# Moving the final normalisation of a fused attention and feed-forward kernel from VectorE to ScalarE and GpSimd, on one core

## The reference, cut to what matters

```python
xn   = layernorm(x)                                        # no gain, no bias
q, k, v = split(xn @ Wqkv + bqkv)
qp, kp  = elu(q) + 1, elu(k) + 1
attn = (qp @ (kp.T @ v)) / (qp @ sum(kp) + 1e-6)           # per sequence
z    = layernorm(xn + attn) * g1 + b1
h    = silu(z @ Wg + bg) * (z @ Wu + bu)                   # 256 -> 682
y    = layernorm(z + h @ Wd + bd) * g2 + b2                # 682 -> 256
gate = silu(scale * (xn @ ternary(W).T))
out  = x + y * gate
```

## Time and profile before

| what | value |
|---|---|
| time, three runs | 1328.03 us median (1326.86, 1328.03, 1335.59) |
| profiled execution, span from first to last instruction | 1331.0 us; its own time is not shown apart from the three above |
| PE / PEld busy | 1285.1 us (97%) / 1152.5 us (87%) |
| DVE busy | 1159.3 us (87%), 2900 instructions |
| ACT busy | 940.7 us (71%) |
| POOL busy | 632.6 us (48%), 683 instructions |
| TensorE clock granted, mean | 0.993 |
| transfers | 41 GB/s over the span |

### The profile page before, as it was taken

How to read it: one execution, slowest core, us unless ns; L and a number is a source line. 1 busy time by engine, 2 the same in 40 slices (tenths; PEclk the granted TensorE clock), 3 DMA queues, 4 the chain that set the end, 5 groups by cost and what they waited for, 6 DMA issues and landing times.

```text
span 1331.0 us, 25237 instructions
## 1 busy us (share of the span) xinstructions
PE 1285.1 (97%) x8147; PEld 1152.5 (87%) x8147; DVE 1159.3 (87%) x2900; ACT 940.7 (71%) x1626; POOL 632.6 (48%) x683
## 2 busy tenths in 40 slices
PE   7889999999999999999999999999999999999995
PEld 5779898898898989889888888888989888988884
DVE  6987888989888988988989888989888988878886
ACT  5697777777777877677777677777677777756641
POOL 4732444554534554544554544554543554533343
PEclk8999999999999999999999999999999999999998
DMA  6200011111011111011111011111001111111100
GB/s 195 80 17 17 1 49 49 49 48 49 9 41 48 49 49 49 6 43 49 49 49 48 17 33 49 49 49 49 23 27 49 49 32 33 33 33 33 33 16 32
DMA packets 57895, 55.81 MB, mean 42 GB/s; under 512 B 5967, under 2 KB 56997, under 8 KB 57766
## 3 DMA queue, kind: packets, MB, share of 16 engines
q1 hardware_dynamic: 57766, 54.20, 12.9%
HBM read 37.41 MB, written 16.78 MB: 41 GB/s over the span
## 4 chain that ended last, share of the span: by engine, by line
PE 76%; DVE 16%; issue 4%; ACT 2%; POOL 1%; DMA 0%; SPq 0%; DVEq 0%; ACTq 0%; POOLq 0%
PE bank L917 57%; PE d_bank L917 14%; DVE rz L803 5%; DVE rz L798 4%; PE xk_bank L917 3%; DVE hs L767 3%; DVE h_l L777 2%; PE bank L931 2%; ACT h_h L476 1%; DMA bk1b<-in_L_attn_bqkv_dram 0%; DVE xn L682 0%; DVE kp L709 0%; POOL rz L318 0%; DVE kp_l L715 0%; POOL rz L320 0%
## 5 line engine op out<-in xcount | busy, mean ns | idle before, releaser
L424 POOL TENSOR_TENSOR rstd<-ve,neg_half 128x4 f32<-128x4 f32 x96 | 100.7, 1049 | 506.1 <-DVE ve L667 506.1
L917 PE MATMUL bank<-zT_h,wgu_h 128*128 128x512 f32 x704 | 280.7, 399 | 0.2 <-DVE zT_l L755 0.2
L917 PE MATMUL bank<-zT_l,wgu_h 128*128 128x512 f32 x704 | 278.7, 396 | 0.0
L917 PE MATMUL bank<-zT_h,wgu_l 128*128 128x512 f32 x704 | 278.7, 396 | 0.0
L476 ACT ACTIVATE hs<-bank,hb 128x512 f32<-128x512 f32 x192 | 131.5, 685 | 116.0 <-DVE h_l L777 79.9
L777 DVE TENSOR_TENSOR h_l<-hs,h_h 128x512 fp32r<-128x512 f32 x160 | 150.6, 944 | 61.9 <-ACT h_h L476 60.7
L917 PE MATMUL d_bank<-wd_h,h_h 128*128 128x256 f32 x640 | 183.7, 287 | 12.5 <-DVE h_l L777 12.5
L318 POOL TENSOR_TENSOR rz<-rz,sg 128x256 f32<-128x256 f32 x126 | 124.8, 990 | 145.9 <-DVE rz L803 145.9
L917 PE MATMUL d_bank<-wd_l,h_h 128*128 128x256 f32 x640 | 180.8, 283 | 0.0
L917 PE MATMUL d_bank<-wd_h,h_l 128*128 128x256 f32 x640 | 180.4, 282 | 0.0
L917 PEld LDWEIGHTS bank<-zT_l,wgu_h 128*128 128x128 f32 x704 | 132.4, 188 | 31.3
(11 more groups left out here) (125 smaller groups left out, 3553.6 us busy)
## 6 DMA issues: line engine op xcount, KB each, us to landing
xa<-in_L_attn_x_dram SPq DMA_DIRECT2D x32, 512.0 KB, 5.7
xq<-in_L_attn_x_dram SPq DMA_DIRECT2D x32, 512.0 KB, 4.9
out_dram<-rz SPq DMA_DIRECT2D x31, 512.0 KB, 3.4
rz<-in_L_attn_Wg_dram SPq DMA_DIRECT2D x1, 640.0 KB, 4.4
rz<-in_L_attn_Wu_dram SPq DMA_DIRECT2D x1, 640.0 KB, 5.4
sg<-in_L_attn_Wd_dram SPq DMA_DIRECT2D x1, 640.0 KB
qp<-in_L_attn_Wqkv_dram SPq DMA_DIRECT2D x1, 512.0 KB, 4.7
out_dram<-rz SPq DMA_DIRECT2D x2, 256.0 KB, 2.1
```

What stands on the lines that cost most here:

```text
L424: eng.tensor_tensor(dst, ve[:, k, :], neg_half[:, 0:1].to_broadcast([P, TILES]), ALU.pow).then_inc(S[f"rs{k}"], 1)
L917: ins = eng.matmul(dst, left, right, start=first and n == 0, stop=last and n == len(pairs) - 1, **kw)
```

## The change

Six things change together.

1. `last_norm` goes. DVE only makes `nmr2` = -mean * rstd for four tiles in one small instruction (`last_shift`), ACT makes row * rstd + nmr2 (`last_rows`, four instructions a group), and GpSimd does the rest in four instructions over the whole group, 128x1024 each: times g2, plus b2, times sg, plus xq (`last_wide`). `z_g1` is now also one 128x1024 instruction.
2. `h_rows` writes the product of chunks 0 to 4 into the PSUM bank of the up job and not into `hs`; `h_high` and `h_low` read it there. So `hs` is free after `h_rows`, and an up bank only after `h_low`.
3. The lists of ACT, DVE and GpSimd change; TensorE's steady list does not.
4. Iteration 31 has its own lists: D is spread between the gate and up jobs.
5. For the last group GpSimd works out sg*b2, sg*g2 and xq + sg*b2 beforehand (`end_terms`), and DVE finishes in two instructions a tile (`end_rows`).
6. The two output transfers of the last group are tiles 0-1 and 2-3, both after DVE.

```diff
 SCALAR_STEPS = steps("""
...
-    k_exp 1, q_high 1, k_exp 2, silu_gate 0, x_res 0, silu_gate 1, h_high 0, k_high 0, x_res 1,
-    silu_gate 2, silu_tern 0, h_high 1, x_res 2, k_exp 3, k_high 1, x_res 3, k_high 2, silu_tern 1,
-    silu_gate 3, k_high 3, xT_high 0, h_high 2, silu_gate 4, xT_high 1, z_rows 0, z_rows 1,
-    h_high 3, z_rows 2, z_rows 3, h_high 4, xn_high 0, silu_gate 5, xn_high 1, h_high 5""")
+    k_exp 1, q_high 1, k_exp 2, silu_gate 0, x_res 0, silu_gate 1, h_high 0, k_high 0, x_res 1,
+    h_high 1, silu_gate 2, silu_tern 0, last_rows 0, last_rows 1, x_res 2, last_rows 2, last_rows 3,
+    k_exp 3, k_high 1, x_res 3, h_high 2, k_high 2, silu_tern 1, silu_gate 3, k_high 3, silu_gate 4,
+    xT_high 0, h_high 3, z_rows 0, z_rows 1, xT_high 1, z_rows 2, z_rows 3, h_high 4, xn_high 0,
+    silu_gate 5, xn_high 1, h_high 5""")
...
 GPSIMD_STEPS = steps("""
-    xn_low 0, z_g1 0, last_rstd 0, xn_low 1, z_g1 1, sum_k 0, a_rstd 0, q_rstd 0, result 0, sum_k 1,
-    z_g1 2, sum_k 2, result 1, result 2, result 3, sum_k 3, z_g1 3""")
+    xn_low 0, z_g1 0, xn_low 1, last_rstd 0, a_rstd 0, sum_k 0, last_wide 0, last_wide 1, q_rstd 0,
+    last_wide 2, sum_k 1, last_wide 3, sum_k 2, sum_k 3""")
+
+END_JOBS = steps("""
+    D 4, D 5, G 0, U 0, G 1, U 1, G 2, D 0, U 2, G 3, D 1, U 3, G 4, D 2, U 4, GU 5, D 3""")
...
+END_VECTOR = steps("""
+    zT_low 0, zT_low 1, ffn_rows 0, ffn_rows 1, ffn_rows 2, ffn_rows 3, last_stats 0, h_rows 0,
+    last_shift 0, h_low 0, h_rows 1, h_low 1, h_rows 2, h_low 2, h_rows 3, h_low 3, h_rows 4, h_low 4,
+    h_rows 5, h_low 5""")
+END_GPSIMD = steps("""
+    z_g1 0, end_terms 0, last_rstd 0, last_wide 0, last_wide 1, last_wide 2, last_wide 3""")
+DRAIN_VECTOR = steps("""
+    ffn_rows 0, ffn_rows 1, ffn_rows 2, ffn_rows 3, last_stats 0, end_rows 0""")
...
-                "U": ("h", HC * g + n + 1), "GU": ("h", HC * g + n + 1),
+                "U": ("hl", HC * g + n + 1), "GU": ("h", HC * g + n + 1),
...
+            def last_wide(g, n):
+                rows = rz[:, g % RZ, :, :]
+                if g == GROUPS - 1:
+                    return
+                if n == 0:
+                    eng.wait_ge(S["n2"], TILES * (g + 1))
+                    eng.tensor_tensor(rows, rows, each_tile(g2b), ALU.mult).then_inc(S["a"], 1)
+                elif n == 1:
+                    eng.wait_ge(S["a"], g + 1)
+                    eng.tensor_tensor(rows, rows, each_tile(b2b), ALU.add).then_inc(S["b"], 1)
+                elif n == 2:
+                    eng.wait_ge(S["b"], g + 1)
+                    eng.wait_ge(S["sg"], PAIRS * (g + 1))
+                    eng.tensor_tensor(rows, rows, sg[:, g % SG, :, :], ALU.mult).then_inc(S["c"], 1)
+                else:
+                    eng.wait_ge(S["c"], g + 1)
+                    eng.tensor_tensor(rows, rows, xq[:, g % 3, :, :], ALU.add).then_inc(S["o"], 1)
...
+            def last_rows(g, t):
+                if g < GROUPS - 1:
+                    eng.wait_ge(S["nm2"], g + 1)
+                    act(rz[:, g % RZ, t, :], rz[:, g % RZ, t, :], ACT.Identity, "n2",
+                        scale=rstd2[:, t:t + 1], bias=nmr2[:, t:t + 1])
...
-                eng.scalar_tensor_tensor(out=hs[0:rows, n % 2, :], in0=up,
+                eng.scalar_tensor_tensor(out=hidden(g, c)[0:rows, :], in0=up,
...
+            def end_rows(g, _=0):
+                eng.wait_ge(S["ag2"], TILES * (g + 1))
+                eng.wait_ge(S["gs"], 1)
+                for t in range(TILES):
+                    row_ = rz[:, g % RZ, t, :]
+                    eng.scalar_tensor_tensor(out=row_, in0=row_, scalar=mv[:, 2, t, 0:1], in1=sg[:, g % SG, t, :],
+                                             op0=ALU.subtract, op1=ALU.mult).then_inc(S["a_last"], 1)
+                eng.wait_ge(S["rs2"], g + 1)
+                eng.wait_ge(S["xb"], 1)
+                for t in range(TILES):
+                    row_ = rz[:, g % RZ, t, :]
+                    eng.wait_ge(S["a_last"], t + 1)
+                    eng.scalar_tensor_tensor(out=row_, in0=row_, scalar=rstd2[:, t:t + 1], in1=xq[:, g % 3, t, :],
+                                             op0=ALU.mult, op1=ALU.add).then_inc(S["o_last"], 1)
```

More of the change, by code:

```diff
@@ L85 @@
     kv_low 0, k_add 2, k_max 0, ffn_rows 0, k_max 1, kv_low 1, ffn_rows 1, q_low 0, ffn_rows 2,
[L86 to L89, removed]
+    ffn_rows 3, q_low 1, k_add 3, last_stats 0, h_rows 0, h_rows 1, h_low 0, last_shift 0, h_low 1,
+    attn 0, attn 1, k_low 0, k_max 2, h_rows 2, a_norm 0, h_low 2, attn 2, k_low 1, attn 3,
+    q_aggregate 0, k_max 3, k_low 2, k_low 3, h_rows 3, attn_norm 0, h_low 3, xT_low 0, h_rows 4,
+    xT_low 1, h_low 4, h_rows 5, h_low 5""")
 GPSIMD_STEPS = steps("""
-    xn_low 0, z_g1 0, last_rstd 0, xn_low 1, z_g1 1, sum_k 0, a_rstd 0, q_rstd 0, result 0, sum_k 1,
-    z_g1 2, sum_k 2, result 1, result 2, result 3, sum_k 3, z_g1 3""")
+    xn_low 0, z_g1 0, xn_low 1, last_rstd 0, a_rstd 0, sum_k 0, last_wide 0, last_wide 1, q_rstd 0,
+    last_wide 2, sum_k 1, last_wide 3, sum_k 2, sum_k 3""")
+END_JOBS = steps("""
+    D 4, D 5, G 0, U 0, G 1, U 1, G 2, D 0, U 2, G 3, D 1, U 3, G 4, D 2, U 4, GU 5, D 3""")
+END_SCALAR = steps("""
+    zT_high 0, zT_high 1, silu_gate 0, h_high 0, silu_gate 1, last_rows 0, h_high 1, last_rows 1,
+    silu_gate 2, last_rows 2, h_high 2, last_rows 3, silu_gate 3, h_high 3, silu_gate 4, h_high 4,
+    silu_gate 5, h_high 5""")
+END_VECTOR = steps("""
[6 more added lines that the diff above has]
+    ffn_rows 0, ffn_rows 1, ffn_rows 2, ffn_rows 3, last_stats 0, end_rows 0""")
 FILL_JOBS = steps("""
@@ L127, in schedule @@
         add("TX", 0, 1)
-    for kind, n in FILL_JOBS if filling(i) else TENSOR_JOBS:
+    for kind, n in order_of(i, FILL_JOBS, TENSOR_JOBS, END_JOBS):
         if kind.startswith("setup_"):
@@ L454, in z_g1 @@
+            def z_g1(g, _):
+                rows = rz[:, g % RZ, :, :]
+                eng.wait_ge(S["TZ"], PAIRS * (g + 1))
                 if g == 0:
                     eng.wait_ge(s_vec, 16 * VECTORS)
-                eng.tensor_tensor(row_, row_, g1b[:, :], ALU.mult).then_inc(S["zg"], 1)
+                eng.tensor_tensor(rows, rows, each_tile(g1b), ALU.mult).then_inc(S["zg"], 1)
             def setup_d_low():
@@ L465, in _ @@
                 a, q, f, last = i + LEAD, i + 1, i, i - 1
-                run_steps(FILL_GPSIMD if filling(i) else GPSIMD_STEPS, {
-                    "xn_low": (a, xn_low), "sum_k": (a, sum_k), "z_g1": (f, z_g1), "result": (last, pool_result),
+                run_steps(order_of(i, FILL_GPSIMD, GPSIMD_STEPS, END_GPSIMD), {
+                    "xn_low": (a, xn_low), "sum_k": (a, sum_k), "z_g1": (f, z_g1), "last_wide": (last, last_wide),
+                    "end_terms": (f, end_terms),
                     "a_rstd": (a + 1, lambda g, _: rstd(0, g, rstd0[:, g % LN0, :])),
@@ L572, in h_high @@
                     dst = ht[0:rows, :]
-                act(dst, hs[0:rows, n % 2, :], ACT.Copy, "hh")
+                act(dst, hidden(g, c)[0:rows, :], ACT.Copy, "hh")
             def xk_copy(g, _):
@@ L646, in _ @@
                     "silu_tern": (q, silu_tern), "xT_high": (a + 1, xT_high), "z_rows": (q, z_rows),
-                    "xn_high": (a + 1, xn_high)})
+                    "xn_high": (a + 1, xn_high), "last_rows": (last, last_rows)})
         @block.vector
@@ L904, in _ @@
                     "q_aggregate": (q, lambda g, _: aggregate(1, g)), "last_stats": (last, last_stats),
-                    "attn_norm": (q, attn_norm), "last_norm": (last, last_norm),
-                    "last_result": (last, last_result), "xT_low": (a + 1, xT_low)})
+                    "attn_norm": (q, attn_norm), "last_shift": (last, last_shift),
+                    "end_rows": (last, end_rows), "xT_low": (a + 1, xT_low)})
                 if i == -1:
```

96 lines of the change are left out of this document (47 added, 49 removed).

## The result

The changed kernel takes 1378.98 us (median of 4 runs, 1376.7 to 1380.34) against 1327.44 us before (4 runs). The ratio is 1.0384, 95% interval 1.0351 to 1.0417. The forecast of 1312 us and its range of 1307 to 1329 are wrong, on the other side. The profiled execution took 1378.72 us and spans 1376.9 from its first to its last instruction.

A forecast was written before the change was run, and what follows sets the result against it. TensorE was taken as the bound, busy 38.85 of 39.28 us per full iteration. The terms -14.3 + 1.3 + 1.8 + 0 - 4.4 = -15.6 took the 1328.0 us median to 1312 us, range 1307 to 1329.

The forecast's parts named there:

- Step 1: Full iterations: D 3 no longer waits for `h_low 3` behind `last_norm`; 26 x 0.55 us, -14.3 us.
- Step 2: Full iterations, what is late next: waits at U 3 and GU 5 both just fit; +1.3 us booked.
- margin of 0.1: At U 3, due at 585.06: `h_low 2` is done at 584.9, so U 3 does not wait, or just.
- rival C: GpSimd's `last_wide 0` starts before DVE's `k_max 2`, so U 3 waits 1.8 + 0.1 us; 1360 us, chance 0.12.
- The walk on ACT: ACT before U 3: with four `last_rows` ahead, `h_high 2` is done near 584.18, ahead of `h_low 2`.
- the 0.35 forecast: At GU 5, due at 592.98: `h_low 3` is done at 592.6 behind a shut-out `attn_norm`, margin 0.35 us.
- A: U 3 or GU 5 misses its margin and waits 0.2 to 0.5 us every iteration; about 1319 us, chance 0.2.
- B: D 3 gets another wait of the same size, so its gap stays; near 1324 to 1326 us, chance 0.1.
- D: GpSimd's wide instructions take 3.0 us, so GU 5 waits 1.3 + 0.1 us; about 1356 us, chance 0.08.
- Step 3: Iterations 27 to 30: GU 5 comes sooner and waits 0.9 us for `h_low 3`; 4 x 0.45, +1.8 us.
- Step 4: Iteration 31: D 0 waits 1.9 us behind rstd, offsetting the new order of D; 0 us.
- Step 5: After the last product: only subtract-and-multiply instructions beside rstd and four more remain; -4.4 us.

The follow-up runs named there:

- e3_wide_late: The changed kernel with GpSimd's `last_wide` 0 and 1 moved behind `q_rstd`; 1311.26 us, ratio 0.9895 to the kernel before.
- e5_best: e3_wide_late with `last_rstd` ahead of `end_terms` in the last group's GpSimd list; 1309.79 us, ratio 0.9898 to the kernel before.
- e4_forms: No kernel: nine DVE instruction forms timed alone and beside GpSimd's 128x1024 `tensor_tensor`; `a_norm`'s form took 411 ns alone, up to 2381 beside it.
- e1_norm_early: The changed kernel with `k_max 2`, `k_low 0` and `a_norm` ahead of `attn 0` on DVE; 1313.84 us, ratio 0.9915 to the kernel before.
- e7_hs_back: e3_wide_late with `h_rows` writing chunks 0 to 4 into `hs` again and the old waits back; 1322.27 us, ratio 0.9993 to the kernel before.

## Why the prediction was wrong

**Step 1, the gap at D 3 goes: right, and a little undersized.** No full iteration has a D that waits for `h_low`. Where nothing else waits, the period is 38.54 (e3_wide_late, e5_best), not 38.7 to 38.8: 0.74 us less, where I had booked 0.55. My own row held most of that: 1.70 - 1.44 = 0.26 for the restart, not 0.1, makes 0.69 with the gap of 0.43. Against that, two of the 25 periods before had no gap, and I had counted 26. Together the steady part gives back 16.8 us (976.5 for 993.3) where 14.3 was forecast.

**Step 2, what is late next: the step that failed,** at the sentence "But `k_max`, `k_low` and the three small `nmr` instructions still have two". I listed the DVE instructions that GpSimd can shut out by one mark, two SBUF operands. `a_norm` has one, so I let it keep its 1.4 us; it took 4.93. It stood between `h_rows 2` and `h_low 2` in the very walk that left U 3 a margin of 0.1. The small `nmr` behind it, which the mark did name, stood there too: rival C lets `last_wide 1` shut it out, the walk gives it no wait. e4_forms shows the mark was too narrow. The Trainium skill, SBUF — State Buffer, section "Who interferes with whom", which I had cited for two inputs, names in the same list copy, cast and `tensor_scalar` as able to contend when their operands meet its conditions; e4_forms agrees, with 2381 ns for 411. The kernel before gave no warning in the median of this instruction (406 ns), but it did in the greatest, 835.

The rest of step 2 came out. The walk on ACT: `h_high 2` ended in time. The race of rival C: `k_max 2` at 606.27 won against `last_wide 0` at 606.29, by 0.02 us. That is close enough to call it luck. Wide instructions: 2.38 to 2.59 in the mean of each line, and 2.4 was taken. `attn_norm` was shut out for 1.77 us, and GU 5 (620.92) did not wait for `h_low 3` (done at 620.39); that margin of 0.5 is no test of the 0.35 forecast, since the wait at U 3 had moved both:

```profile
618.02 1.77 DVE L800 SCALAR_TENSOR_TENSOR nmr<-mv,rstd 128x4 f32<-128x4 f32 x1
619.71 0.68 DVE L828 TENSOR_TENSOR h_l<-bank,h_h 128x512 fp32r<-128x512 f32 x1
```

**Rivals.** C had the right wait (U 3), the right mechanism and nearly the right size (1.8 + 0.1 for 2.16), but hung it on a race that was won. It priced 1360. Of the 19 us up to 1379, some 8.5 are the larger gap (42.0 + 1.5 for 35) and 7.8 the clock, which no case of mine had; the later first G 0 and the distance from the median to the profile give 7 more, and iterations 27 to 30 take 5.6 off. A, B and D did not occur.

**Step 3, iterations 27 to 30: wrong in sign.** I booked +1.8; they gave 3.8 back (32.0 for 32.74 three times, 29.25 for 30.79). The ring has five places: without the two TX jobs the job five before GU 5 is N 3 and no longer U 3, so GU 5 doesn't need `h_low 3`. I moved the due time and forgot that the partner moves too.

**Step 4, iteration 31: right.** D 0 waits 2.1 us behind rstd, as the row shows (forecast 1.9). From G 0 to `ve` behind the last product it is 29.5 us for 28.9, where 0 more was forecast.

```profile
1349.88 0.16 DVE L849 SCALAR_TENSOR_TENSOR nmr<-mv,rstd 128x4 f32<-128x4 f32 x1 [2.67 <-POOL rstd L436]
```

**Step 5, the end: right.** From `ve` to the last result 1374.24 - 1370.90 = 3.3 us where it was 8.0; -4.4 was forecast.

```profile
1370.90 0.17 DVE L718 TENSOR_SCALAR ve<-mv 128x4 f32<-128x4 f32 x1
1370.97 1.67 DVE L858 SCALAR_TENSOR_TENSOR rz<-rz,mv,sg 128x256 f32<-128x256 f32 x4
1372.57 1.67 DVE L865 SCALAR_TENSOR_TENSOR rz<-rz,rstd,xq 128x256 f32<-128x256 f32 x4
```

So the sum of 1312 lies near e3_wide_late (1311.26) and e1_norm_early (1313.84), kernels with a few steps elsewhere. That it lies so near is in part luck: from the profile before, e3_wide_late is 19.8 us shorter (full iterations -16.8, 27 to 30 -3.7, the rest -3.2, a first G 0 3.9 later), where I had forecast 15.6 from a median that lies lower. The failed term is the one put at nothing: `a_norm` beside `last_wide`.

## What to carry to other kernels

Before making a GpSimd instruction wider, write down every DVE instruction that can run beside it and sort them as e4_forms does, by whether a PSUM operand is among them and not by the number of SBUF inputs. Of the forms tried, each one without it but the statistics was held for up to the GpSimd instruction's whole length, and all behind it on DVE waits too. Then ask what stands behind such a step that TensorE waits for, and move one of the two. When a margin is a tenth of the work in front of it, price each instruction in that work at its worst, not at its median. And when a phase has fewer jobs in a ring of buffers, work out again who waits for whom.

## What the hardware showed that I had not expected

- A `tensor_scalar` with two per-partition scalars takes 0.41 us for 128x256 from SBUF to SBUF, with a constant 0.29; both are shut out. Into or out of PSUM the first takes 0.54 and is never shut out. A tiny one, 128x4, took up to 2.27 us.
- Right behind a wait of 2.15 us in an otherwise full TensorE the granted clock fell to 0.50 for 3.4 us (0.62 over 4.4 us) in 5 of 25 iterations, each the one after an iteration with KV jobs. The sixth of these and the others, with the same gap, were not slowed. Why those five is open.
- A PE that is busy for a whole stretch is not always at its shortest: e7_hs_back has 38.78 of 38.78 busy, where e3_wide_late needs 38.54 for the same products.
